# Transfers that pack each head's attention output into full rows, one output product per token tile, and the second norm behind ACT's other work of its slot

## What is computed

```
xn = _layernorm(x)
# first attention, per head h (8 features): q, k with rotary positions
scores = q @ k.T * scale + bias(distance), causal
probs  = softmax(scores)
elastic = relu(probs + tau[h] / row)
out[:, 8h:8h+8] = elastic @ v
x = x + out @ Wo.T + fp4_ffn(xn)          # silu(gate) * up, then down
xn = _layernorm(x)                        # the second norm
x = x + linear_attention(xn) @ w_out + experts(xn)
```

## Time and profile before

| | us |
|---|---|
| median of 3 runs | 2231.35 |
| lowest and highest | 2228.76, 2233.91 |
| the profiled execution | 2231.71 |
| its span, first to last instruction | 2229.9 |
| TensorE busy | 2045.9 (92%) |
| DVE busy | 1571.6 (70%) |
| ACT busy | 1443.9 (65%) |
| POOL busy | 1152.9 (52%) |

### The profile page before, as it was taken

The page is one execution under the profiler, slowest core; times in us unless marked ns, Lnnn a source line. Parts: engine busy times, 40 slices in busy tenths (PEclk is TensorE's granted clock), DMA queues, the critical chain, the costliest instruction groups (busy, mean ns, idle before and its releaser), DMA issues.

```text
span 2229.9 us, 52509 instructions
## 1 busy us (share of the span) xinstructions
PE 2045.9 (92%) x18761; PEld 1367.5 (61%) x18761; DVE 1571.6 (70%) x5288; ACT 1443.9 (65%) x3925; POOL 1152.9 (52%) x1800
## 2 busy tenths in 40 slices
PE   3789999999999999989999999998989999898989
PEld 2455666756566575666656566575656657566655
DVE  7557767677676867767677776867777686775745
ACT  1767576666757757576675757667585675757542
POOL 5675463745636455463745637465463745535220
PEclk9779999999999999999999999999999999999999
DMA  4000000000000000000000000000000000000000
GB/s 124 6 6 2 1 15 2 16 2 9 8 2 15 1 16 1 2 16 1 16 1 11 6 2 16 2 16 2 2 16 2 15 2 11 2 2 11 2 10 6
DMA packets 33542, 22.03 MB, mean 10 GB/s; under 512 B 2443, under 2 KB 32771, under 8 KB 33283
## 3 DMA queue, kind: packets, MB, share of 16 engines
q1 hardware_dynamic: 33283, 18.68, 2.9%
HBM read 14.48 MB, written 4.19 MB: 8 GB/s over the span
## 4 chain that ended last, share of the span: by engine, by line
PE 64%; DVE 16%; ACT 9%; issue 6%; POOL 4%; DVEq 0%; ACTq 0%; POOLq 0%
PE ps L1114 11%; PE ps L1254 8%; PE ps L1195 7%; PE ps L1185 7%; PE ps L1128 6%; PE ps L1104 4%; DVE ring L542 3%; PE ps L1083 3%; ACT ring L925 3%; PE ps L1173 2%; PE ps L1239 2%; ACT pb L934 2%; PE ps L1212 2%; PE ps L1161 2%; PE ps L1224 2%
## 5 line engine op out<-in xcount | busy, mean ns | idle before, releaser
L817 POOL TENSOR_SCALAR ring<-ring,row_rcp,tau_row 128x128 f32<-128x128 f32 (+3 forms) x1024 | 629.3, 622 | 737.5 <-DVE row_rcp L549 737.5
L925 ACT ACTIVATE ring<-ring,neg_max 128x128 f32<-128x128 f32 (+3 forms) x1024 | 571.0, 559 | 491.3 <-DVE neg_max L542 486.9
L1114 PE MATMUL ps<-identf,ring 128*128 128x128 f32 x2560 | 382.7, 287 | 13.4 <-POOL ring L817 7.4
L934 ACT ACTIVATE pb<-ps 128x512 f32<-128x512 f32 x640 | 348.3, 584 | 30.4 <-PE ps L1114 26.4
L542 DVE CUSTOM_DVE_ANT_1 ring<-ps,bias_t 128x384 f32<-128x384 f32 (+1 forms) x496 | 287.0, 615 | 68.4 <-PE ps L1104 60.5
L1114 PEld LDWEIGHTS ps<-identf,ring 128*128 128x128 f32 x2560 | 277.4, 143 | 92.6 <-issue 41.8
L1254 PEld LDWEIGHTS ps<-ed_t,h 128*128 128x128 f32 (+1 forms) x1920 | 252.1, 191 | 82.9 <-issue 81.2
L1254 PE MATMUL ps<-ed_t,h 128*128 128x128 f32 (+1 forms) x1920 | 272.4, 278 | 0.0
L1185 PE MATMUL ps<-xn1T,eg_t 128*128 128x512 f32 (+1 forms) x480 | 256.5, 616 | 1.8 <-DVE h L596 1.6
L1195 PE MATMUL ps<-xn1T,eu_t 128*128 128x512 f32 (+1 forms) x480 | 256.1, 615 | 1.7 <-DVE h L603 1.7
L948 ACT ACTIVATE tanh_t<-ps 128x512 f32<-128x512 f32 (+2 forms) x304 | 172.2, 566 | 125.0 <-PE ps L1185 121.3
(11 more groups left out here) (162 smaller groups left out, 3202.2 us busy)
## 6 DMA issues: line engine op xcount, KB each, us to landing
x_t<-x SPq DMA_DIRECT2D x16, 256.0 KB, 2.8
x<-x SPq DMA_DIRECT2D x16, 256.0 KB, 2.9
out<-x SPq DMA_DIRECT2D x16, 256.0 KB, 2.5
bias_t<-bias SPq DMA_DIRECT2D x1, 1536.0 KB, 7.7
eg_t<-eg SPq DMA_DIRECT2D x1, 860.0 KB
eu_t<-eu SPq DMA_DIRECT2D x1, 860.0 KB
ed_t<-ed SPq DMA_DIRECT2D x2, 320.0 KB
ring<-inv_row SPq DMA_DIRECT2D x1, 256.0 KB, 2.7
```

Source lines behind the costliest of these rows:

```text
L817: pool.tensor_scalar(e, e, row_rcp[:, m % 2, r:r + 1], tau_row[:, i, HG * g + r:HG * g + r + 1], ALU.mult, ALU.add).then_inc(p_ok.sem, 1)
L925: act.activation(e, e, ACT.Exp, bias=neg_max[:, n % 2, r:r + 1], scale=-1.0, accum_out=row_sum[:, n % 2, r:r + 1]).then_inc(exp_ok.sem, 1)
L934: act.activation(pb[:, c % NPB, :], bank(turn_bank(q)), ACT.Relu).then_inc(t_taken[q % 2].sem, 1)
L1114: last = pe.transpose(o[:, r * P:(r + 1) * P], ring_of(i, r)[:, k * P:(k + 1) * P], idf)
```

## The change

The 8 rows of each head are gathered by transfers into `o_rows`, where they stand in the order of the features (partition 8h for head h), so that the output product needs the plain weight `wo_t` and is one for each token tile. It stands where the product of group 3 stood. The padded weight and its load go. `o_stack` keeps two groups instead of four, and `store_o` waits for the transfers of the group two before. SP now goes through the slots as the other engines do, and issues four transfers (8 rows of 2 KB) after each group. On ACT the second norm leaves `beside` and is issued behind all other work of its slot.

```
+            def pack_o(b, g):
+
+                sp.wait_ge(os_ok.sem, os_ok.at(b, g + 1))
+                if g == 0 and b:
+                    sp.wait_ge(y_ps.sem, y_ps.at(b - 1, 1))
+                for r in range(HG):
+                    h = HG * g + r
+                    sp.dma_start(o_rows[HD * h:HD * (h + 1), :], o_stack[R * r:R * r + HD, g % 2, :]).then_inc(or_ok[g % 2].sem, 16)
...
+STORE_Y = L1 + 70
+PACK_O = tuple(ATT + NS * (g + 1) + 9 for g in range(G))
...
-            for f in range(-1, NB + 2):
-                if has(f + 2):
-                    sp.wait_ge(xn_ok[0].sem, xn_ok[0].at(f + 1, T))
-                    load(f + 2)
-                if has(f - 2):
-                    store(f - 2)
-                    if has(f - 1):
-                        sp.wait_ge(y_out.sem, y_out.at(f - 2, 16))
-                        load_residual(f - 1)
+            for f, s in plan.slots():
+                for b, p in plan.beside(f, s):
+                    if p == 3 and has(b + 1):
+                        sp.wait_ge(xn_ok[0].sem, xn_ok[0].at(b, T))
+                        load(b + 1)
+                    if p in PACK_O:
+                        pack_o(b, PACK_O.index(p))
+                    if p == STORE_Y:
+                        store(b)
+                    if p == STORE_Y + 1 and has(b + 1):
+                        sp.wait_ge(y_out.sem, y_out.at(b, 16))
+                        load_residual(b + 1)
...
             def store_o(b, g):
                 act.wait_ge(pv_ps.sem, pv_ps.at(b, BLOCKS_TO[T * (g + 1)]))
-                if g == 0 and b:
-                    act.wait_ge(y_ps.sem, y_ps.at(b - 1, 1))
-                act.copy(o_stack[:, g, :], bank(PV)).then_inc(os_ok.sem, 1)
+                if G * b + g >= 2:
+                    act.wait_ge(or_ok[g % 2].sem, 16 * HG * (G // 2 * b + g // 2))
+                act.copy(o_stack[:, g % 2, :], bank(PV)).then_inc(os_ok.sem, 1)
...
             def beside(b, p):
                 if p == 2:
                     norm(b, 0, x_t, xn)
-                if p == ADD_X1 + 3:
-                    if has(b + 2):
-                        act.wait_ge(t_ps.sem, plan.turn["xq", b + 2, 0] + 1)
-                    norm(b, 1, x1, xn1)
...
                 for b, p in plan.beside(f, s):
                     beside(b, p)
+                for b, p in plan.beside(f, s):
+                    if p == ADD_X1 + 3:
+                        if has(b + 2):
+                            act.wait_ge(t_ps.sem, plan.turn["xq", b + 2, 0] + 1)
+                        norm(b, 1, x1, xn1)
...
             def attention_out(b, t):
 
                 if t == 0:
-                    pe.wait_ge(os_ok.sem, os_ok.at(b, G - 1))
                     pe.wait_ge(s_taken.sem, plan.score["fy", b, 0] + 1)
-                ts = slice(t * P, (t + 1) * P)
-                o = bank(Y)[:, t * D:(t + 1) * D]
                 if t < T - 1:
-                    pe.matmul(o, tau_future[:, ts], y_future[:, t, :], start=False, stop=False)
-                for g in range(G - 1):
-                    pe.matmul(o, o_stack[:, g, ts], wo_pad_t[:, g, :], start=False, stop=False)
+                    pe.matmul(bank(Y)[:, t * D:(t + 1) * D], tau_future[:, t * P:(t + 1) * P], y_future[:, t, :], start=False, stop=False)
 
             def attention_out_last(b):
-                pe.wait_ge(os_ok.sem, os_ok.at(b, G))
+                for k in range(2):
+                    pe.wait_ge(or_ok[k].sem, or_ok[k].at(b + 1, 0))
                 for t in range(T):
-                    last = pe.matmul(bank(Y)[:, t * D:(t + 1) * D], o_stack[:, G - 1, t * P:(t + 1) * P], wo_pad_t[:, G - 1, :],
+                    last = pe.matmul(bank(Y)[:, t * D:(t + 1) * D], o_rows[:, t * P:(t + 1) * P], wo_t[:, :],
                                      start=False, stop=(t == T - 1))
```

More of the change, by code:

```diff
@@ L158, in blocks_before, with build @@
         return [blk for back in (4, 2) for blk in self.blocks(*divmod(SLOTS * f + s - back, SLOTS))]
-def build(nc, x, wq, wk, wv, wo, wo_pad, bias, tau, tau_col_in, wg, wu, wd, wqkv1, wout1, eg, eu, ed,
+def build(nc, x, wq, wk, wv, wo, bias, tau, tau_col_in, wg, wu, wd, wqkv1, wout1, eg, eu, ed,
           cos, sin, ident, tri, inv_row, inv_col, head_mask, head_of, suffix, sel, lower, out):
@@ L193, in build @@
         wo_t = sb("wo_t", [P, D])
-        wo_pad_t = sb("wo_pad_t", [P, G, D])
         wgq = sb("wgq", [P, 384])
@@ L239, in build @@
         pb = sb("pb", [P, NPB, HG * P])
-        o_stack = sb("o_stack", [P, G, L])
+        o_stack = sb("o_stack", [P, 2, L])
+        o_rows = sb("o_rows", [P, L])
         lin = sb("lin", [P, NLIN, T, P])
@@ L324, in build @@
         os_ok = signal("o_stack_ready", G)
+        or_ok = two("o_rows_ready", 16 * HG * G // 2)
         exp_ok = signal("exp_with_sum", NS * HG)
@@ L348, in build @@
         ]
-        consts_late = [(bias_t[:, 1:1 + H, 64:256], bias), (wo_t[:, :], wo), (wo_pad_t[:, :, :], wo_pad)]
+        consts_late = [(bias_t[:, 1:1 + H, 64:256], bias), (wo_t[:, :], wo)]
         consts_layer1 = [
@@ L1366 @@
     wo = a["L0_attn_Wo"].T
-    wo_pad = np.zeros((G, HG, R, D), np.float32)
-    wo_pad[:, :, 0:HD, :] = wo.reshape(G, HG, HD, D)
     s = lambda e, w: np.concatenate([a[f"L1_ffn_{e}"], a[f"L1_ffn_{w}"][None]], 0)
@@ L1371 @@
         "x": a["L0_attn_x"], "wq": a["L0_attn_Wq"].T, "wk": a["L0_attn_Wk"].T, "wv": a["L0_attn_Wv"].T,
-        "wo": wo, "wo_pad": wo_pad.transpose(1, 2, 0, 3).reshape(P, G, D), "bias": bias, "tau": a["L0_attn_tau"],
+        "wo": wo, "bias": bias, "tau": a["L0_attn_tau"],
         "tau_col_in": np.concatenate([a["L0_attn_tau"], np.zeros(P - H, np.float32)])[:, None],
```

## The result

The changed kernel takes 2175.03 us, the median of four runs from 2174.82 to 2175.10, against 2231.76 us for the kernel before beside it. The ratio is 0.9747 with a 95% interval of 0.9730 to 0.9763: faster by 2.5%. The forecast was 2173 us.

What follows compares the result with a forecast made beforehand. TensorE, busy 92% of the span, was taken as the bound. Packing 28.1, last two frames 2.3, norm 15.4 and clock 12.3 summed to 58.1 us off 2231.7, giving 2173 us on the median's scale; range 2155 to 2194.

Steps and rivals of the forecast that it cites:

- Part 1, the packing: Output products, frames 1 to 14: three removed products count 2.0 us a frame, slot 11's counts nothing; 28.1 us.
- TensorE alone decides: Rival, chance 0.16: ACT's lack of gaps in slots 11 to 15 gives way, all removed products count; 2156 us.
- Part 2, the norm: Slot 16 on ACT: tanh ahead of the second norm shortens TensorE's slot-18 wait; 1.1 us a frame, 15.4 us.
- Clock: Half-speed products behind the 2.36 us wait of slot 18, in 7 of 14 frames, vanish: 12.3 us.
- The last two frames: Frames 15 and 16, where TensorE has no next item and waits for transfers: 1.8 and 0.5, together 2.3 us.
- The transfers: SP's four 16 KB transfers per group: no cost in frames 1 to 14, with 2.2 to 3.2 us of room.
- The clock still falls: Rival, chance 0.14: half speed returns after two shorter waits in the same place; 12.3 us less gain, 2186 us.
- Part 1 given back: Rival, chance 0.10: ACT's row of slots 11 to 16 returns the packing's gain; 28 us remain, 2204 us.
- The last group lands too late: Rival, chance 0.05: TensorE stands in slot 12 every frame, slower from an 8.7 us landing; 2253 us at 10 us.

Runs made afterwards that it cites:

- e2: The changed kernel with the second norm put back where it was, so only the packing and fewer output products remain: 2197.92 us, ratio 0.9856.
- e3: The changed kernel with three products of the removed size, against a tile of zeros, put back in slot 7 of each frame: 2186.51 us.
- e4: The changed kernel with three products of the removed size, against a tile of zeros, put back in slot 11 instead: 2175.95 us.
- e1: The kernel before with only the second norm moved behind the other work of ACT's slot 16: 2204.49 us, ratio 0.9885.
- e8: The changed kernel with two idle 128x512 copies on ACT ahead of the tanh of gate tile 2, frames 1 to 14: 2195.98 us.
- e7: The changed kernel with the third and fourth gate tile of the first FFN one slot earlier (15, 17): 2162.36 us, ratio 0.9683.
- e10: The kernel with the two gate tiles one slot earlier, unchanged, run again for comparison on another chip: 2163.83 us.
- e6: The changed kernel with two more transfers of the same size, to a spare tile, ahead of those of group 3: 2178.89 us.
- e5: The changed kernel with four more transfers of the same size, to a spare tile, ahead of those of group 3: 2187.39 us.
- e9: The kernel with two gate tiles one slot earlier, plus ACT issuing two of group 3's four transfers in frames 15 and 16: 2161.72 us.

## Why the prediction was right, and where it was not

**Part 1, the packing.** 2.0 us a frame forecast, 2.03 measured in e2. That slots 7 to 9 pay in full and slot 11 not at all was the choice that kept the forecast from the 2156 us of "TensorE alone decides", and e2, e3 and e4 show both halves of it. One sentence in it was wrong: I read the 0.29 us between ACT's copy and the weight load in the earlier trace rows as room of which TensorE could keep 0.2 to 0.3. It was the hand-over itself: the changed kernel shows 0.28 us with TensorE waiting. There was no room, and the value of nothing that I took for other reasons was right.

**Part 2, the norm.** 1.1 us a frame forecast, 1.14 in e1. The wait shrank by 1.52 us (2.36 to 0.84) where I had 1.54. The turn of the norm's result gave some of it back: it starts 0.97 us behind the gate product (1210.46 to 1211.43) and not 0.70 as in the earlier trace rows, so 0.27 us of it. In all the frame gives back 1.52 - 1.14 = 0.38 us, where I had 0.4.

**Clock.** 12.3 us forecast, 11.8 us found in the 13 frames. The cause is shown by e1, e2 and e8. For the last two frames I had reckoned with no change of the clock, and they are the term that was off:

**The last two frames.** 2.3 us forecast. The changed kernel's stretch from the last gate product of slot 18 to the end is 0.3 us shorter, and some 0.4 of the norm's give-back in frame 14 lie in it, so about 0.7 us. Of the missing 1.6 us, 0.9 are lost ahead of the output products of frame 15 and 0.7 behind them. From the first issue to TensorE's start it is 4.15 us, which lies between the 3.4 and 4.4 us that I had from the end of the copy. But I had the copy in frame 15 come 0.67 us earlier, because three products ahead of it are gone. It doesn't. The timeline of the changed kernel in frame 15:

```profile
1966.38 0.62 ACT L941 ACTIVATE ring<-ring,neg_max 128x384 f32<-128x384 f32 x1 [0.75 <-DVE neg_max L558]
...
1968.07 0.57 ACT L956 COPY o_stack<-ps 128x512 f32<-128x512 f32 x1
...
1972.83 1.13 PE L1242 MATMUL ps<-wo_t,o_rows 128*128 128x128 f32 x8 [1.50 <-DMA o_rows<-o_stack]
```

From the last gate product of slot 18 to the end of this copy it is 1968.64 - 1857.04 = 111.60 us, where the kernel before has 2024.66 - 1913.48 = 111.18. The 0.4 us more are the norm's give-back, and nothing is gained beside it: the exponential two steps ahead of the copy, which DVE releases after 0.75 us in both kernels, starts 109.34 us behind that gate product here and 108.92 us before. So TensorE waits 1.50 us where I had 0.4 to 1.4, and its output products are 0.9 us earlier (the give-back set aside) where I had taken 1.8.

The rest goes with the clock. The timeline of windows shows it, first of the kernel before, then of the changed one, last of e2, all three behind the output products of frame 15:

```profile
2036.00:2040.00 4.00, 2.03 (x14) 1.24 (x18) 0.57 (x7) 4.00 (x14) 2.83 (x4) 0.86 0.02 6
2040.00:2044.00 4.00, 4.00 (x36) 2.78 (x28) 1.24 (x7) 2.46 (x7) 1.32 (x3) 0.71 0.00 0
```

```profile
1978.00:1982.00 4.00, 1.68 (x11) 1.10 (x10) 0.88 (x9) 3.88 (x13) 3.75 (x5) 0.83 0.02 6
1982.00:1986.00 4.00, 4.00 (x38) 3.00 (x37) 0.96 (x5) 2.38 (x7) 1.31 (x3) 0.50 0.00 0
1986.00:1990.00 4.00, 4.00 (x19) 2.43 (x18) 2.35 (x13) 2.02 (x7) 1.39 (x2) 0.82 0.00 0
```

```profile
2005.00:2009.00 4.00, 3.83 (x38) 3.16 (x39) 0.90 (x5) 2.98 (x10) 1.70 (x4) 0.64 0.00 0
2009.00:2013.00 4.00, 4.00 (x20) 2.39 (x18) 2.83 (x14) 2.45 (x9) 1.87 (x3) 0.93 0.00 0
```

By (1 - clock) x 4 us that is 1.7 us of lost clock before, 3.4 us in the changed kernel and 1.7 us in e2. Yet e2 has the same waits for the transfers as the changed kernel, 1.49 and 2.17 us. So the wait of 1.50 us by itself doesn't bring the added 1.7 us at this place. What the added half clock costs shows in the time from the output products of frame 15 to those of frame 16: 119.23 us in the changed kernel, 118.13 in e2, 118.51 before. In frame 16 it is the other way round: e2 loses 6.8 us of clock and the changed kernel 5.1, and from the output products to the end e2 takes 82.12 us and the changed kernel 81.14.

Over frames 15 and 16 together the lost clock, summed in the same way, is 5.1 us in e1 and 6.8 in the kernel before, which have no waits for transfers. It is 8.5 in the changed kernel and in e2, e4, e7, e8 and e10, 10.2 in e3, and 11.9 and 12.0 in e6 and e5, whose waits are the longest. But it is 3.4 in e9, which has one wait of 1.2 us. So longer waits mostly go with more half clock there, but not strictly, and what decides it in a given frame stays open.

**The transfers.** They cost nothing in frames 1 to 14, as forecast, with room of 2.5 us where I had 2.2 to 3.2. The path to it was wrong twice, and the errors cancelled, which was luck. An issue of this kind takes 0.67 us and not the 0.37 of a residual's load in the earlier trace rows. That isn't because it stands behind another: the first of a group already shows 0.65 us (at 1194.14), while the constants' loads at the start, issued in a row, take 0.43 us each for the most part. And TensorE starts 2.1 us behind the start of the last issue (1073.00 to 1075.08 in e5), where I had 0.37 for that issue and 2.9 for the landing. The rule against many small transfers, named in the forecast from the Trainium skill's page "DMA: Bandwidth & Descriptors", was not tried, since no run sends the same rows in fewer transfers. In the last two frames, where nothing covers them, four transfers of 16 KB cost TensorE 1.5 and 2.2 us; in the others they cost nothing. The 2.0 us that the same page of the Trainium skill gives for the fixed part of a transfer issued by GpSimd is near the 2.1 us found here for SP.

**The rivals.** "TensorE alone decides" falls with e4. "The clock still falls" falls in frames 1 to 14, but e8 shows how near it was: at 1.88 us it would have been partly true. "Part 1 given back" falls with e2. "The last group lands too late" is real at a delay of 2.5 us and more, as e5 shows, and there it begins gently.

## What to carry to other kernels

A product removed from the busiest engine is worth its full price only where the next thing it does doesn't wait for another engine; ask it slot by slot, and put a dummy of the same size back to see it. A short step of another engine that frees a buffer should stand ahead of a longer one in the same slot, if both are ready and the longer one is needed later. A wait of about 2 us on TensorE should be priced with what the lower clock costs behind it.

## What the runs showed that I had not expected

- The runs of the kernel before spread over 5 us, from 2228.76 to 2233.91, those of the changed kernel over 0.3 us. The falls behind the wait of slot 18 don't explain it: e2, with five of them, spreads over 1.3 us, and e1 and e7, with none, over 2.3 and 2.2 us.
- SP's issues of 8 rows of 2 KB within the on-chip memory take 0.67 us each, where the issue of a 256 KB load from main memory shows 0.37 us.
- Putting the two gate tiles one slot earlier (e7) is worth another 0.5 to 0.6%: its frame takes 128.3 us, 0.9 less, near the 1.14 us of the norm's place.
